# Row normalisations done batch by batch inside the neighbouring loops of a four-layer graph kernel

## The reference

```
x = layernorm(x + L0(x, adj, ...))        # diffusion, 8 Euler steps
x = layernorm(x + L1(x, adj, W, a))       # attention over the graph
x = layernorm(x + L2(x, adj, W1, b1, W2, b2))   # filter in the eigenbasis U of the Laplacian
x = layernorm(x + L3(x, ..., src, dst))   # attention over 256 edges
# layernorm(x) = (x - mean) / sqrt(var + 1e-5) over the last axis
# L2: relu((U.T x) W1 + b1) W2 + b2, then U times that
# L3: per edge a score from two gathered projections, softmax over edges of one source, scatter, W_out
```

## Time and profile before

| | us |
|---|---|
| median of 3 runs | 4145.84 |
| lowest and highest | 4143.9, 4145.85 |
| the profiled execution's own time | 4153.18 |
| its span | 4151.4 |
| TensorE busy | 2843.8 (69%) |
| VectorE busy | 3157.0 (76%) |
| ScalarE busy | 864.7 (21%) |
| GpSimd busy | 1218.4 (29%) |

### The profile page before, as it was taken

One profiled execution on the slowest core, in us unless ns is written; L12 is line 12 of the kernel. 1 busy time (PEld: TensorE's weight loads), 2 busy tenths in 40 slices (PEclk: granted clock), 3 DMA queues, 4 the chain that ended last, 5 costly groups with the idle time before them and its releaser, 6 DMA issues. The chain is left out here.

```text
span 4151.4 us, 77402 instructions
## 1 busy us (share of the span) xinstructions
PE 2843.8 (69%) x21043; PEld 2136.5 (51%) x21043; DVE 3157.0 (76%) x18105; ACT 864.7 (21%) x3720; POOL 1218.4 (29%) x5211
## 2 busy tenths in 40 slices
PE   4778778777776666665558667748496446769694
PEld 3666666666654545444448434425353225646662
DVE  4888888888888888888873788899999548942463
ACT  1212222222223333333320001001010002321201
POOL 1554555555555555555550111000000000000000
PEclk8555555555555555555555778879798668889868
DMA  1000000000000000000011000000000000000001
GB/s 59 2 2 2 2 2 2 2 2 2 2 2 2 1 2 1 1 1 1 1 55 32 1 1 1 1 1 0 0 1 0 0 0 0 0 0 0 0 1 41
DMA packets 23019, 23.83 MB, mean 6 GB/s; under 512 B 3024, under 2 KB 21328, under 8 KB 22096
## 3 DMA queue, kind: packets, MB, share of 16 engines
q1 hardware_dynamic: 22608, 19.17, 1.4%
HBM read 14.97 MB, written 4.19 MB: 5 GB/s over the span
## 5 line engine op out<-in xcount | busy, mean ns | idle before, releaser
L373 PE MATMUL h_sums<-h_P,ones 128*128 128x60 f32 (+3 forms) x1020 | 315.3, 404 | 244.3 <-DVE h_P L559 165.8
L831 PE MATMUL d_acc<-d_h,U 128*128 128x512 f32 x1024 | 471.4, 604 | 0.0
L381 PE MATMUL h_axp<-h_XV,ident 128*128 128x64 f32 x1018 | 337.2, 435 | 184.4 <-POOL h_XV L425 184.4
L354 PE MATMUL h_sums<-h_parts,ones 128*128 128x19 f32 (+2 forms) x1020 | 315.5, 399 | 188.0 <-DVE h_parts L512 163.0
L373 PEld LDWEIGHTS h_sums<-h_P,ones 128*128 128x128 f32 x1020 | 255.0, 310 | 304.9 <-issue 304.9
L362 PE MATMUL h_axp<-h_XV,x 128*128 128x4 bf16 x11514 | 388.5, 169 | 17.0 <-DVE h_CX L523 16.5
L354 PEld LDWEIGHTS h_sums<-h_parts,ones 128*128 128x128 f32 x1020 | 256.7, 312 | 273.9 <-DVE h_parts L512 234.1
L381 PEld LDWEIGHTS h_axp<-h_XV,ident 128*128 128x128 f32 x1018 | 254.4, 310 | 267.4 <-DVE h_y L597 218.3
L411 POOL TENSOR_TENSOR h_root<-urow,h_halves 128x1 f32<-128x1 f32 x510 | 278.1, 545 | 380.2 <-DVE urow L564 380.2
L362 PEld LDWEIGHTS h_axp<-h_XV,x 128*128 128x128 bf16 x11514 | 362.6, 105 | 33.9 <-DVE h_CX L523 25.4
L831 PEld LDWEIGHTS d_acc<-d_h,U 128*128 128x128 f32 x1024 | 188.8, 195 | 202.2 <-issue 202.2
(11 more groups left out here) (566 smaller groups left out, 6975.9 us busy)
## 6 DMA issues: line engine op xcount, KB each, us to landing
cut<-in_c_cut SPq DMA_DIRECT2D x1, 4608.0 KB, 14.0
x<-in_x SPq DMA_DIRECT2D x16, 256.0 KB, 4.3
out<-x SPq DMA_DIRECT2D x16, 256.0 KB, 3.6
adj<-in_adj SPq DMA_DIRECT2D x1, 1024.0 KB, 5.2
below<-in_c_below SPq DMA_DIRECT2D x1, 1024.0 KB, 7.3
neps<-in_c_neps SPq DMA_DIRECT2D x1, 1024.0 KB, 8.4
UT<-in_c_ramp SPq DMA_DIRECT2D x1, 1024.0 KB, 10.3
same<-in_c_same SPq DMA_DIRECT2D x1, 448.0 KB, 9.9
```

The costliest lines, as they stand in the source:

```text
L354: nc.tensor.matmul(PS1[:, lo:hi], m.ones[:], parts[:, lo:hi], start=True, stop=True).then_inc(sums_ready, 1)
L373: nc.tensor.matmul(PS2[:, :, T1 * c0:], m.ones[:], P2[:, :, c0:, :].rearrange("p i c t -> p i (c t)"), start=True, stop=True).then_inc(pv_ ...
L381: nc.tensor.matmul(sides(PSE), m.ident[:, r:r + 1].broadcast_to([P, P]), sides(XV[:, cr, 0:2 * RIGHT]), start=True, stop=True).then_inc(ro ...
L831: i = nc.tensor.matmul(acc, m.mixT[:, c, r * P:(r + 1) * P], src[:, :, c, :], start=False, stop=(c == C - 1), skip_group_check=True)
```

## The change

`Norm` stays at the start of `attend` alone. A new class `RowNorm` normalises one batch: `moments` (4 BN_STATS and seven operations on 4 columns, on VectorE), `root` (the power -0.5, on GpSimd) and `scale` (4 row scalings, on VectorE). The norm behind attention is done inside the filter's loop, two batches ahead; the norm behind the filter inside the first edge loop, three batches ahead; and the last one inside the second edge loop, one and two batches behind, each batch's store waiting only for that batch. The copies `f_xs` and `e_xs` go: TensorE reads x itself. The filter's loop and VectorE's part of both edge loops, and TensorE's gather loop, are written out for all 16 batches.

```diff
+class RowNorm:
+    def moments(self, dve, b):
+        v, st = self.nc.vector, self.stats
+        mean, diff, var = (self.col[:, b % 2, i, :] for i in range(3))
+        do = Steps(dve, self.step, b * 3)
+        for c in range(C):
+            t = v.bn_stats(st[:, c, :], self.m.x[:, b, c, :])
+        do(t)
+        v.tensor_tensor(mean, st[:, :, 1], st[:, :, 4], ALU.add)
+        v.tensor_tensor(diff, st[:, :, 1], st[:, :, 4], ALU.subtract)
+        do(v.tensor_tensor(var, st[:, :, 2], st[:, :, 5], ALU.add))
+        v.tensor_scalar(mean, mean, 0.5, None, ALU.mult)
+        v.tensor_scalar(var, var, 1.0 / F, 1e-5, ALU.mult, ALU.add)
+        do(v.tensor_tensor(diff, diff, diff, ALU.mult))
+        v.scalar_tensor_tensor(var, diff, 0.25, var, ALU.mult, ALU.add).then_inc(self.var_ready, 1)
+    def root(self, pool):
+        for b in range(B):
+            pool.wait_ge(self.var_ready, b + 1)
+            self.nc.gpsimd.tensor_tensor(self.col[:, b % 2, 3, :], self.col[:, b % 2, 2, :], self.minus_half[:],
+                                         ALU.pow).then_inc(self.root_done, 1)
+    def scale(self, dve, b):
+        mean, rstd = self.col[:, b % 2, 0, :], self.col[:, b % 2, 3, :]
+        dve.wait_ge(self.root_done, b + 1)
+        for c in range(C):
+            x = self.m.x[:, b, c, :]
+            t = self.nc.vector.tensor_scalar(x, x, mean[:, c:c + 1], rstd[:, c:c + 1], ALU.subtract, ALU.mult)
+        t.then_inc(self.normed, 1)
...
 def filter_spectrum(nc, m):
...
-                pe.wait_ge(staged, b + 1)
+                pe.wait_ge(norm.normed, b + 1)
                 after(pe, agg_taken, b - 1)
...
+            norm.begin()
+            for b in range(2):
+                norm.moments(dve, b)
+                norm.scale(dve, b)
+            for b in range(B):
+                if b + 2 < B:
+                    norm.moments(dve, b + 2)
                 dve.wait_ge(o_ready, b + 1)
                 after(dve, y_ready, b - 1)
-                v.tensor_tensor(o[:, u], op[:], bias, ALU.add).then_inc(o_taken, 1)
-                if not isinstance(b, int) or b > 0:
-                    finish(b - 1, 1 - u)
-            norm.vector(dve)
+                v.tensor_tensor(o[:, b % 2], op[:], bias, ALU.add).then_inc(o_taken, 1)
+                if b + 2 < B:
+                    norm.scale(dve, b + 2)
+                if b:
+                    finish(b - 1)
...
 def edge_attend(nc, m, out):
...
         def _(sp):
-            sp.wait_ge(norm.dve_part, 1)
             for b in range(B):
-                if b * C == norm.SPLIT:
-                    sp.wait_ge(norm.act_part, 1)
+                sp.wait_ge(close.normed, b + 1)
                 sp.dma_start(out[b].rearrange("(c p) f -> p c f", p=P), m.x[:, b]).then_inc(stored, 16)
...
             def transpose(b):
-                pe.wait_ge(staged, b + 1)
+                pe.wait_ge(norm.normed, b + 1)
...
+            norm.begin()
+            close.begin()
+            for b in range(3):
+                norm.moments(dve, b)
+                norm.scale(dve, b)
             v.tensor_copy(rowf[:], m.edge_row[:])
...
-            with dve.Fori(0, B) as b:
+            for b in range(B):
                 lp = Steps(dve, step, b * PER_A + base)
+                if b + 3 < B:
+                    norm.moments(dve, b + 3)
                 dve.wait_ge(gath_ready, b + 1)
...
                 lp(v.tensor_tensor(t2[:], t2[:], m.w["L3_gnn_a"][:].unsqueeze(1).broadcast_to([P, Q, F]), ALU.mult))
+                if b + 3 < B:
+                    norm.scale(dve, b + 3)
...
             def finish(b):
                 dve.wait_ge(y_ready, b + 1)
-                v.tensor_tensor(x, x, yp[:], ALU.add).then_inc(y_taken, 1)
-            batches(dve, message, B - 1)
+                v.tensor_tensor(m.x[:, b], m.x[:, b], yp[:], ALU.add).then_inc(y_taken, 1)
+                dve.wait_ge(y_taken, b + 1)
+                close.moments(dve, b)
+            for b in range(B):
+                message(b)
+                if b > 1:
+                    close.scale(dve, b - 2)
+                if b:
+                    finish(b - 1)
+            close.scale(dve, B - 2)
             finish(B - 1)
-            dve.wait_ge(y_taken, B)
-            norm.vector(dve)
+            close.scale(dve, B - 1)
```

More of the change, by code:

```diff
@@ L1499, in _ @@
             batches(act, batch, B - 1)
-            norm.scalar(act)
         @block.vector
@@ L1573, in filter_spectrum, with _, aggregate, spread @@
         yp = ctx.enter_context(nc.psum_tensor("f_y_ps", [P, 2, C, F], F32))
-        norm = Norm(nc, ctx, m, "f_norm")
+        norm = RowNorm(nc, ctx, m, "f_norm")
         block = ctx.enter_context(nc.Block())
-        whole = lambda b: m.x[:, b] if isinstance(b, int) else m.x[:, bass.ds(b, 1), :, :].rearrange("p o c f -> p (o c) f")
+        @block.gpsimd
+        def _(pool):
+            norm.root(pool)
         @block.tensor
         def _(pe):
-            def aggregate(b, u):
-                pe.wait_ge(staged, b + 1)
+            def aggregate(b):
+                pe.wait_ge(norm.normed, b + 1)
                 after(pe, agg_taken, b - 1)
                 for c in range(C):
-                    t = nc.tensor.matmul(aggp[:, u, :], xs[:, u, c, :], m.U[:, c, :], start=(c == 0), stop=(c == C - 1))
+                    t = nc.tensor.matmul(aggp[:, b % 2, :], m.x[:, b, c, :], m.U[:, c, :], start=(c == 0), stop=(c == C - 1))
                 t.then_inc(agg_ready, 1)
-            def spread(b, u):
+            def spread(b):
                 pe.wait_ge(o_taken, b + 1)
@@ L1608, in batch @@
                 t.then_inc(o_ready, 1)
-            aggregate(0, 0)
-            batches(pe, batch, B - 1)
-            spread(B - 1, (B - 1) % 2)
+            spread(B - 1)
         @block.scalar
         def _(act):
[L1616 to L1622, removed]
+            for b in range(B):
                 act.wait_ge(agg_ready, b + 1)
                 after(act, hid_ready, b - 1)
-                nc.scalar.activation(agg[:, u, :], aggp[:, u, :], ACT.Copy).then_inc(agg_taken, 1)
+                nc.scalar.activation(agg[:, b % 2, :], aggp[:, b % 2, :], ACT.Copy).then_inc(agg_taken, 1)
                 act.wait_ge(hid_ready, b + 1)
@@ L1628, in batch @@
                 nc.scalar.activation(hid[:], hidp[:], ACT.Relu, bias=m.w["L2_gnn_b1"][:]).then_inc(hid_taken, 1)
-            stage(0, 0)
-            batches(act, batch, B - 1)
-            norm.scalar(act)
         @block.vector
@@ L1755, in _ @@
             transpose(1)
-            batches(pe, gather, B - 1)
+            for b in range(B):
+                gather(b, b % 2)
             pe.wait_ge(ready, 1)
```

72 lines of the change are left out of this document (36 added, 36 removed).

## The result

The changed kernel takes 4180.11 us in the median of 4 runs (4175.55 to 4181.34), the kernel before on the same chip 4145.78 (4143.9 to 4145.85). The forecast was 4170 with a range to 4188. The profiled execution after took 4181.34 with a span of 4179.3, which is 27.9 more than the span before, 4151.4.

A forecast was written before the change was run, and what follows sets the result against it. It took TensorE to bound the filter, whole VectorE norms the seams, and an engine chain the second edge loop. Terms summed to +8.0 at unchanged clock, +24 with clock losses; 4145.84 + 24 = 4170 us, range 4148 to 4188.

The forecast's parts named there:

- Part 1: The norm behind attention goes; TensorE's first `aggregate` comes at 3663.84 instead of 3685.65: 21.8 us less.
- Part 2: Filter's loop: `aggregate` waits for `scale` behind the bias addition, 2.08 us in each of 14 rounds: 29.1 more.
- Parts 3 and 4: The norm behind the filter goes, 25.2 us less; three batches' norms stand first in the edge prologue, 11.9 more.
- Part 5: First edge loop: TensorE's transposes wait for `scale`, 1.46 us in each of 13 rounds: 19.0 more.
- Part 6: Second edge loop: `moments` between addition and message, rounds of 5.80 us, 23.6 more; with the tail, 5 less in all.
- The clock in the second edge loop: TensorE's granted clock falls to 0.75 as its busy part shrinks: 0.96 us a round, 13.4 more in all.
- a difference carries over: The +24 us, summed in the profiled execution, was added to the kernel before's median of 4145.84, giving 4170.
- A: Second edge loop: same mechanism, but TensorE's clock stays at 0.98; sum +8, 4154 us; chance 0.17.
- B: Clock 0.5 throughout the second edge loop, 0.9 in the filter: 27 + 10 us above forecast, 4207; chance 0.05.
- C: VectorE's pieces on the path each 0.2 us dearer or cheaper: 9 us, 4161 or 4179; chance inside the forecast's 0.57.
- D: Second edge loop: GpSimd's root holds the message, 14 us more, 4184; chance 0.05.
- E: A wait counted in the filter or first edge loop is covered, worth 29 or 19 us; change faster; chance 0.08.

The follow-up runs named there:

- x1: Changed kernel with the four scalings of batch b+2 moved ahead of the bias addition in the filter's loop: 4150.53 us, ratio 1.0001 to the kernel before.
- x2: Changed kernel with the first edge loop's norms moved behind the score reduction and further ahead: 4159.99 us, ratio 1.0025 to the kernel before.
- x9: Changed kernel with three extra, unused TensorE products behind each projection of the second edge loop: 4155.95 us, ratio 1.0019 to the kernel before.
- x3: Changed kernel with the second edge loop's message put ahead of the last norm's moments and scalings: 4126.37 us, ratio 0.995 to the kernel before.
- x7: Changed kernel with the masks and weights put ahead of the three norms in the edge prologue: 4164.43 us, ratio 1.0038 to the kernel before.
- x6: Changed kernel with only BN_STATS between addition and message in the second edge loop, the rest of `moments` behind the message: 4158.09 us, ratio 1.0017.
- x5: Changed kernel with the last norm done whole behind the second edge loop, as before: 4161.3 us, ratio 1.0029 to the kernel before.

## Why the prediction was right, and where its size was off

The direction and the mechanism held: each of the three loops waits for VectorE at the place that the prediction named. The steps one by one:

- Part 1, forecast -21.8, came to -22.6. The second batch was ready in time, as said.
- Part 2, +29.1, with 3 more for the clock. The round is 10.83 for 10.84, x1 gives back 30.8. But the clock stayed where it was, so its 3 did not come; the 1.7 above 29.1 lie at the start, where batch 2's `aggregate` is partly at the low clock and lasts 5.40 instead of 3.70. That part is of this execution: most others with the same loop don't have it (x1).
- Parts 3 and 4, -13.3 together at the seam, came to -13.5. The prologue behind it was 2.3 shorter, which the prediction had at nothing: its first projection takes 1.99 instead of 3.65, as the clock has risen by then, the conversion of the edge list 0.42 instead of 0.88, and the picks 9.65 instead of 9.86.
- Part 5, +19.0, came to +18.3, and x2 shows that it is this wait.
- Part 6 without the clock: 5.80 a round; x9 measures 5.82 with TensorE kept at work. The tail came 2.2 sooner, since a store that is alone lands earlier.
- **The clock in the second edge loop is the term that was mis-sized.** The prediction took a granted clock of 0.75, which was nearly right (0.73), and made 0.96 a round of it, 13.4 in all. Measured is (106.8 - 14 x 5.80) / 14 = 1.83 a round, 25.6 in all, and x9 takes 106.8 - 81.4 = 25.4 of it away between the same additions. The step that failed is "2.87 / 0.75 - 2.87": it divides the work by the mean clock of the stretch. The mean includes the idle time, in which the clock is worth nothing. TensorE works for 2.87 + 1.83 = 4.70 of a round of 7.63, which is 2.87 / 4.70 = 0.61 while it works, and leaves (0.73 x 7.63 - 2.87) / 2.93 = 0.92 while it waits; the trace's own clock, taken over the busy and the idle parts of these 14 rounds, is 0.60 and 0.93. The low level falls onto the work: the median scatter product is 1061 ns, near the long end of 592 to 1222. Why it falls there, and not onto the waits, is not shown.

That the sum missed by so little is partly luck. The clock of the last loop was 12.2 too small, and 9.1 of that was met by terms that came out lower than forecast: the filter with its clock 1.4, the prologue 2.3, the end 2.2, the first edge loop, the filter's start and the seam together 1.7, and 1.5 ahead of the change, which is no effect of it.

Of the missing 10 us between 4170 and 4180.11 the sum accounts for 4.2 only, since between the two profiled executions the difference is 4181.34 - 4153.18 = 28.2 and not 24. The rest is the step "a difference carries over": the profiled execution before lay 7.4 over the median of its four runs, the one after 1.2. Beside the experiments the kernel before ran 51 times, between 4143.06 and 4153.31, with none between 4146.6 and 4149.7 and a median of 4150.64; the median of four runs is that uncertain. Against 4150.64 the changed kernel is 29.5 slower, close to the 27.9 of the spans.

The rivals: A (the clock holds, 4154) fell with 0.73. B had the loop at 0.5 throughout and the filter at 0.9; the loop lost 12 more than forecast, not 27, and the filter nothing. Of the rivals it was the nearest for the loop, though the forecast was a little nearer (25.6 came, 13.4 and 40 were said), and its bound of 40 does hold what came. C: pieces on the path were within 0.06 a round of their rows. D: the message lasted 0.42 as before beside a root that started 0.16 after it. The root lasted 1.12 in these 14 rounds, or 0.11 more than the 1.01 of the roots with no message beside them, where one held to the message's end would have lasted 0.26 more; the path saw none of it. That C's 4179 and D's 4184 lie near the measured time is chance, since neither mechanism came. E: no wait was covered, though x1, x2, x3 and x7 show that each could have been.

## What to carry to other kernels

When a stage of its own is cut into pieces that go into a loop, each piece is free only where its engine has room and nobody is waiting for what it queues up: put the operation that releases the other engine first and the new work behind it, even if its result is used one batch later. Where a change adds a wait to every round of a short loop of TensorE, price all its products at the low clock as a bound (40 us here, of which 25.6 came), and do not divide by the mean clock of the stretch. Before a term is called hidden, ask what stands next in line on the same engine.

## What the runs showed of the hardware

- The length of a single wait does not tell what the clock does. Read from the first round to the last of each loop, 1.8 idle in 10.8 is at 1.00 (filter), 1.2 ahead of the transposes in 7.1 at 1.00 (first edge loop), 1.2 in 4.1 at 1.00 (the kernel before) and 1.1 in 4.0 (x3), but 2.0 in rounds of 4.9 to 6.7 at 0.79 (x6) and 2.9 in 7.6 at 0.73. What decides between 1.2 and 2.0 idle in these short rounds was not tried.
- Nor does TensorE's busy time: between the two edge loops of the kernel before, from 4000 to 4048, its records fill 43.95 of 48 us with products of 64 partitions by 256 columns, and the clock is 0.50. No run here tried why.
- Useless products can pay: three of 0.9 us a round, whose result nobody reads, brought 25 us in sixteen rounds (x9). Work that doesn't wait is better: x3 gains twice as much without any.
- A store of 256 KB lands in 2.2 us when the stores come one at a time, 3.6 when sixteen are issued in a row (x5 and the kernel before).
